# First layer of a four-layer attention program: the maximum ahead of the other VectorE work of its step, and statistics, inverse root, masks and input splits cut up and moved to other steps

## What is computed

```
def _masked_instance_norm(x, mask):
    m = mask.astype(x.dtype)
    x = x * m
    n_valid = jnp.sum(m, axis=-1, keepdims=True)
    mean = jnp.sum(x, axis=-1, keepdims=True) / n_valid
    var = jnp.sum(x * x, axis=-1, keepdims=True) / n_valid - mean * mean
    x = (x - mean) / jnp.sqrt(jax.nn.relu(var) + EPS)
    return x * m
q, k, v = Wq x + bq, Wk kv + bk, Wv kv + bv        (per batch, split into 16 heads)
attn = softmax over the valid keys of (q * scale) k
mean = attn v;  ex2 = attn (v * v);  std = sqrt(relu(ex2 - mean * mean))
out = (masked_instance_norm(x) * std + mean) * mask
```

## Time and profile before

| | us |
|---|---|
| median of 3 runs | 4968.74 |
| the 3 runs | 4964.92 to 4970.57 |
| the profiled execution, its own time | 4961.53 |
| its span, first to last instruction | 4959.9 |
| first layer in that span, to the first transfer of the second | about 955 |
| TensorE busy in the span | 4443.2 (90%) |
| VectorE, ScalarE, GpSimd busy | 3016.6, 1930.0, 1658.7 |

### The profile page before, as it was taken

One profiled execution on the slowest core, in us unless ns is written; L12 is line 12 of the kernel. 1 busy time (PEld: TensorE's weight loads), 2 busy tenths in 40 slices (PEclk: granted clock), 3 DMA queues, 4 the chain that ended last, 5 costly groups with the idle time before them and its releaser, 6 DMA issues. The chain is left out here.

```text
span 4959.9 us, 72439 instructions
## 1 busy us (share of the span) xinstructions
PE 4443.2 (90%) x22864; PEld 3277.2 (66%) x22864; DVE 3016.6 (61%) x6430; ACT 1930.0 (39%) x3756; POOL 1658.7 (33%) x1103
## 2 busy tenths in 40 slices
PE   6999999578888888767999999999999999999986
PEld 3444444255666666545879779787787887888864
DVE  5555555146666766635757567576675766757642
ACT  2444444211222222114545435454254552555511
POOL 1222223234444444322232442333433334333340
PEclk8999998778899889878999999999999999999999
DMA  1000000200000000002222231222312122221123
GB/s 36 23 18 27 18 18 14 98 5 9 14 14 1 14 14 9 9 9 89 63 71 63 66 101 56 78 61 64 98 61 77 61 68 74 72 73 57 57 68 116
DMA packets 126289, 240.90 MB, mean 49 GB/s; under 512 B 16884, under 2 KB 38132, under 8 KB 124896
## 3 DMA queue, kind: packets, MB, share of 16 engines
q1 hardware_dynamic: 123744, 229.50, 14.7%
q0 software_dynamic: 2304, 8.39, 0.4%
HBM read 220.79 MB, written 16.78 MB: 48 GB/s over the span
## 5 line engine op out<-in xcount | busy, mean ns | idle before, releaser
L1790 POOL TENSOR_TENSOR c_wl<-c_wr,c_wh 128x512 fp32r<-128x512 f32 (+1 forms) x576 | 822.6, 1440 | 1674.3 <-ACT c_wh L2102 1466.5
L1355 POOL TENSOR_TENSOR b_sb<-b_sb,b_rt 128x1024 f32<-128x1024 f32 x128 | 285.0, 2226 | 490.1 <-DVE b_sb L1395 490.1
L2196 ACT ACTIVATE c_pr<-c_ps,c_nms 128x257 f32<-128x257 f32 x512 | 244.2, 477 | 477.1 <-DVE c_nms L2390 475.0
L572 ACT ACTIVATE a_ex<-a_ps 128x1024 f32<-128x1024 f32 x256 | 261.2, 1023 | 346.3 <-PE a_ps L408 346.0
L1395 DVE TENSOR_TENSOR_SCAN b_sb<-b_wt,b_s,b_ps 128x256 f32<-128x256 f32 x512 | 355.8, 731 | 11.7 <-issue 4.0
L666 DVE TENSOR_REDUCE a_nm<-a_ps 128x2 f32<-128x1024 f32 x256 | 310.8, 1218 | 76.2 <-PE a_ps L385 73.2
L1849 PE MATMUL c_ps<-c_hh,c_wh 128*128 128x512 f32 x768 | 318.8, 415 | 35.2 <-POOL c_hl L1796 35.2
L1849 PE MATMUL c_ps<-c_gh,c_wh 128*128 128x512 f32 x768 | 307.3, 400 | 20.5 <-DVE c_gl L2428 17.5
L2102 ACT ACTIVATE c_wh<-c_wr 128x512 fp32r<-128x512 f32 (+1 forms) x464 | 316.4, 688 | 9.1 <-PE c_ps L1851 7.5
L1849 PE MATMUL c_ps<-c_wh,c_cth 128*128 128x256 f32 x1024 | 304.6, 297 | 9.3 <-DVE c_ctl L2343 5.0
L1851 PE MATMUL c_ps<-c_hh,c_wl 128*128 128x512 f32 x768 | 310.9, 405 | 0.0
(11 more groups left out here) (306 smaller groups left out, 10925.0 us busy)
## 6 DMA issues: line engine op xcount, KB each, us to landing
c_wr<-in_downs SPq DMA_DIRECT2D x192, 256.0 KB, 2.6
c_wr<-in_wv SPq DMA_DIRECT2D x64, 512.0 KB, 3.9
c_wr<-in_wk SPq DMA_DIRECT2D x128, 256.0 KB, 2.9
c_wr<-in_wq SPq DMA_DIRECT2D x128, 256.0 KB, 2.6
c_wr<-in_fc SPq DMA_DIRECT2D x64, 256.0 KB, 2.8
b_w<-in_w SPq DMA_DIRECT2D x8, 1024.0 KB, 13.1
a_x<-in_x SPq DMA_DIRECT2D x8, 512.0 KB, 3.4
a_ctx<-in_ctx SPq DMA_DIRECT2D x8, 512.0 KB, 4.1
```

The lines of the kernel that those rows point to most:

```text
L572: act.activation(EX[:, n % 4, :, :], ps[:, BT + 2 * (n % 2):BT + 2 * (n % 2) + 2, :], ACT.Exp).then_inc(ex_ready, 1)
L1355: pool.tensor_tensor(SB[:, quad % 3, :, 0:L], SB[:, quad % 3, :, 0:L], RT[:, scan % 2, q // 4, :].unsqueeze(1).broadcast_to([P, 4, L]), AL ...
L1790: pool.tensor_tensor(piece(WL, slot), piece(WR, slot), piece(WH, slot), ALU.subtract).then_inc(piece_cut[slot], 1)
L2196: act.activation(PR[:, i, 0:L + 1], ps[:, BS + 1 - i % 2, 0:L + 1], ACT.Exp, bias=NMS[:, i:i + 1], scale=float(K2) ** -0.5, accum_out=RS[: ...
```

## The change

It has five parts, all in `layer0`. The computation is the same.

1. **Order in a step on VectorE.** `take_max` comes first in every step, ahead of `turned_maxima`.
2. **Statistics.** `moments` keeps only the two operations that read PSUM and stands at step 0 of group 3, before `take_max`; the four that follow become `spread_of_x`, at the end of that step.
3. **Inverse root and spread.** `inverse_root` leaves step 5 of group 0 and is cut in two halves of 128 columns, at step 7 of group 0 and step 0 of group 1. GpSimd multiplies by the spread (`spread_out`, now with a wait of its own on `std_ready`) before it multiplies by the inverse root (`scale`). The lift to zero is done group by group.
4. **Masks.** `mask_rows` moves from step 0 of group 1 to steps 5 and 6 of group 0, half the columns each; the count becomes `count_valid`, at step 1 of group 1; `mask_x` moves from step 5 of group 1 to its step 7 and step 0 of group 2.
5. **Input halves.** One pair of signals for x and ctx becomes two pairs. ScalarE rounds x at step 7 of group 0 and ctx at step 0 of group 1 (before: steps 0 and 1 of group 1). GpSimd takes the low half of x, then scales, then the low half of ctx, then shifts and masks. The projection of queries waits for x alone, that of keys for ctx and the mask row.

The diff, cut to its core:

```diff
-            def cut_low(b):
-
-                pool.wait_ge(xc_high, b + 1 + AHEAD)
+            def cut_x(b):
+
+                pool.wait_ge(x_high, b + 1 + AHEAD)
                 pool.sem_inc(passed, 1)
-                pool.tensor_tensor(XL[:, :, :], X[:, :, :], XH[:, :, :], ALU.subtract)
-                pool.tensor_tensor(CL[:, :, :], C[:, :, :], CH[:, :, :], ALU.subtract).then_inc(xc_low, 1)
+                pool.tensor_tensor(XL[:, :, :], X[:, :, :], XH[:, :, :], ALU.subtract).then_inc(x_low, 1)
+
+            def cut_c(b):
+                pool.wait_ge(c_high, b + 1 + AHEAD)
+                pool.sem_inc(passed, 1)
+                pool.tensor_tensor(CL[:, :, :], C[:, :, :], CH[:, :, :], ALU.subtract).then_inc(c_low, 1)
                 pool.drain().then_inc(inputs_read, 1)
...
-                if g == G0 - 1:
-                    pool.tensor_scalar(VAR[:, :, :], VAR[:, :, :], 0.0, None, ALU.max).then_inc(var_v, 1)
-                    pool.drain()
+                pool.tensor_scalar(VAR[:, :, cols], VAR[:, :, cols], 0.0, None, ALU.max).then_inc(var_v, 1)
...
             def spread_out(b):
+                pool.wait_ge(std_ready, b + 1 + AHEAD)
+                pool.sem_inc(passed, 1)
                 pool.tensor_tensor(XM[:, :, :], XM[:, :, :], VAR[:, :, :], ALU.mult)
...
-            def group_0(b, prior):
+            def group_0(b, prior, more=True):
                 copy_values(b, 1)
                 if prior is not None:
                     group_moments(prior, G0 - 1)
-                    finish_batch(prior)
-
-            def group_1(b, prior, more=True):
+                    spread_out(prior)
                 if more:
-                    cut_low(b + 1)
+                    cut_x(b + 1)
+                if prior is not None:
+                    scale(prior)
+                if more:
+                    cut_c(b + 1)
+
+            def group_1(b, prior):
+                if prior is not None:
+                    shift(prior)
+                    mask_out(prior)
                 copy_values(b, 2)
                 group_moments(b, 0)
...
                 if g == 0:
-                    pe.wait_ge(xc_high, b + 1 + AHEAD)
-                    pe.wait_ge(xc_low, b + 1 + AHEAD)
-                    pe.wait_ge(mask_ready, b + 1 + AHEAD)
+                    pe.wait_ge(x_low, b + 1 + AHEAD)
...
                 it = b * G0 + g
+                if g == 0:
+                    pe.wait_ge(c_low, b + 1 + AHEAD)
+                    pe.wait_ge(mask_ready, b + 1 + AHEAD)
...
-            def group(b, g, left=3, prior=None, first=False):
+            def group(b, g, left=3, prior=None, first=False, more=True):
                 it = b * G0 + g
                 for n in range(NT):
                     act.wait_ge(t_ps, it * NT + n + 1 + AHEAD)
...
                     if g == 1 and left > 2 and n == 0:
-                        cut_x(b + 1)
-                    if g == 1 and left > 2 and n == 1:
                         cut_c(b + 1)
...
                     if g == 0 and n == 5 and prior is not None:
                         roots(prior)
+                    if g == 0 and n == 7 and more:
+                        cut_x(b + 1)
...
-                act.wait_ge(var_v, b + 1 + AHEAD)
+                act.wait_ge(var_v, (b + 1) * G0 + AHEAD)
...
+            def mask_rows(b, half):
+
+                cols = slice(half * L, (half + 1) * L)
+                if half == 0:
+                    dve.wait_ge(inputs_in, (b + 1) * N_IN + AHEAD)
+                    dve.wait_ge(k_ps, b * G0 + AHEAD)
+                mm = dve.tensor_scalar(MBRR[:, cols], M8R[:, cols], -NEG, NEG, ALU.mult, ALU.add)
+                if half == 1:
+                    mm.then_inc(mask_ready, 1)
+
+            def count_valid(b):
                 dve.tensor_reduce(NV[:, :], M8R[:, :], AX.X, ALU.add)
                 dve.drain().then_inc(mask_read, 1)
...
+            def mask_x(b, half):
+
+                if half == 0:
+                    dve.wait_ge(stats_x_in, (b + 1) * N_STATS + AHEAD)
+                    dve.wait_ge(out_ready, b + AHEAD)
+                    dve.tensor_copy(MCOL[:, :], M8C[:, :])
+                    dve.drain()
+                for c in range(2 * half, 2 * half + 2):
                     dve.tensor_scalar(XM[:, c, :], XT[:, c, :], MCOL[:, c:c + 1], None, ALU.mult)
-                dve.drain().then_inc(stats_in, 1)
-                dve.sem_inc(stats_read, 1)
+                if half == 1:
+                    dve.drain().then_inc(stats_in, 1)
+                    dve.sem_inc(stats_read, 1)
...
             def moments(b):
@@ -712,6 +731,8 @@
                 dve.tensor_scalar(ST[:, 0, :], ps[:, BX, 0:L], RN[:, 0:1], None, ALU.mult)
                 dve.tensor_scalar(ST[:, 1, :], ps[:, BX, L:2 * L], RN[:, 0:1], None, ALU.mult)
                 dve.drain().then_inc(st_read, 1)
+
+            def spread_of_x(b):
                 dve.tensor_tensor(ST[:, 2, :], ST[:, 0, :], ST[:, 0, :], ALU.mult)
                 dve.drain()
                 dve.tensor_tensor(ST[:, 2, :], ST[:, 1, :], ST[:, 2, :], ALU.subtract)
@@ -719,14 +740,14 @@
                 dve.tensor_scalar(ST[:, 2, :], ST[:, 2, :], 0.0, None, ALU.max).then_inc(var_x, 1)
                 dve.reciprocal(RN[:, :], NV[:, :])
...
-            def group(b, g, left=3, prior=None, first=False):
+            def group(b, g, left=3, prior=None, first=False, more=True):
                 for n in range(NT):
-                    if g == 1 and left > 2 and n == 0:
-                        mask_rows(b + 1)
+                    if g == G0 - 1 and n == 0:
+                        moments(b)
+                    if left > 1:
+                        take_max(*after(b, g, 2), n)
                     if left and n == TURN_AT:
                         turned_maxima(*after(b, g))
-                    if left > 1:
-                        take_max(*after(b, g, 2), n)
                     if n == OLD_PAIR_AT and not first:
                         if g > 0:
                             take_moments(b, g - 1, 1)
@@ -742,18 +763,35 @@
                         take_moments(b, g, 0)
                     if left and g == G0 - 1 and n == VALUES_AT[1]:
                         take_values(b + 1, 1)
-                    if g == 1 and n == 5:
-                        mask_x(b)
-                    if g == 2 and n == STATS_AT:
-                        moments(b)
-                    if g == 0 and n == 5 and prior is not None:
-                        inverse_root(prior)
-
-            def inverse_root(b):
-                dve.wait_ge(std_ready, b + 1 + AHEAD)
-                dve.reciprocal(ST[:, 3, :], ST[:, 3, :]).then_inc(rstd_ready, 1)
-
-            mask_rows(0)
+                    if g == 0 and n == 5 and more:
+                        mask_rows(b + 1, 0)
+                    if g == 0 and n == 6 and more:
+                        mask_rows(b + 1, 1)
+                    if g == 0 and n == 7 and prior is not None:
+                        inverse_root(prior, 0)
+                    if g == 1 and n == 0 and prior is not None:
+                        inverse_root(prior, 1)
+                    if g == 1 and left > 2 and n == 1:
+                        count_valid(b + 1)
+                    if g == 1 and n == 7:
+                        mask_x(b, 0)
+                    if g == 2 and n == 0:
+                        mask_x(b, 1)
+                    if g == G0 - 1 and n == 0:
+                        spread_of_x(b)
+
+            def inverse_root(b, half):
+                cols = slice(half * P, (half + 1) * P)
+                if half == 0:
+                    dve.wait_ge(std_ready, b + 1 + AHEAD)
+                mm = dve.reciprocal(ST[:, 3, cols], ST[:, 3, cols])
+                if half == 1:
+                    mm.then_inc(rstd_ready, 1)
+
```

53 lines of the change are left out of this document (24 added, 29 removed).

## The result

| | before | after |
|---|---|---|
| median of 4 runs each, us | 4967.81 (4964.92 to 4970.57) | **4860.61** (4855.27 to 4862.44) |
| ratio, 95% interval | | 0.9782 [0.9767, 0.9796] |
| profiled execution, us | 4961.53 | 4855.27 |
| its span, us | 4959.9 | 4853.4 |
| from the span's start to the first product of the second layer, us | 958.27 | 851.26 |

The kernel is 107 us faster. I had forecast 4876 in a range of 4862 to 4944. All of the gain lies in the first layer: it is 107.0 us shorter in the profiled executions, whose whole spans differ by 106.5.

A forecast was written before the change was run, and what follows sets the result against it. TensorE was taken as the bound, losing time to idle moments and a slow clock; 19.4 + 55.5 + 15 + 3 = 93 us off the median of 4968.7 gave 4876 us, range 4862 to 4944.

The forecast's parts named there:

- 29 short waits: TensorE's waits for VectorE's maximum, mostly 0.72 us in step 2 and 0.57 in step 1 of group 3, go: 19.4 us.
- six hand-overs: Step 7 of group 0 and steps 0 to 3 of group 1 get shorter by 9.2 us, six times: 55.5 us.
- last hand-over: Seven steps go from 30.03 to 16.8 us at full clock; with step 7, 15 us less.
- end of the layer: GpSimd's lift by quarters and the inverse root beside the spread at the layer's end: 3 us less.
- The maximum first: In plain steps, VectorE's maximum starts earlier and the copy fits in idle time, so the 0.72 us gaps go.
- A gap of about 1.1 us remains, from ScalarE: In step 7 of group 0 TensorE still waits for ScalarE's exponential; step 7 takes 3.25 us against 5.26.
- The clock stays up: Likeliest case: the 1.1 us gap brings no slow stretch at the hand-overs, 4876 us; chance 0.58.
- it falls at some: Rival: the clock falls at three or four of seven hand-overs, each costing 8.4 us, about 4906; chance 0.14.
- Both rivals on the clock: Clock still falls at every hand-over, 4941 us, chance 0.19; or at three or four of seven, about 4906, chance 0.14.
- What VectorE must do: Mask row, count, inverse root and mask of x, now beside full-clock steps, counted as nothing; bound 3.5 us.
- The case in which an inverse root waits for GpSimd: Its second half waits for the low half of x; maximum of step 1 0.6 us late, 4 us over seven hand-overs.
- The slower rival: TensorE's projection of keys waits 7.4 us at seven hand-overs for GpSimd's low half of ctx: 4993 us; chance 0.03.

The follow-up runs named there:

- e1: The kernel before with part 1 alone, take_max ahead of turned_maxima in every step: 4940.19 us, ratio 0.9949.
- e4: The changed kernel with turned_maxima ahead of take_max again: 4886.38 us, ratio 0.9843 to the kernel before.
- The sweep: The changed kernel with one, two or three small ScalarE copies behind the roots, lengthening the gap in step 7: 4903.36, 4904.83 and 4917.79 us.
- e2: The kernel before with only the whole inverse root moved from step 5 of group 0 to step 7: 4971.45 us, ratio 1.0021.
- e9: The changed kernel with the whole mask row and the count at step 0 of group 1: 4894.12 us, ratio 0.9853 to the kernel before.
- e14: The changed kernel with two more products, later overwritten, in each batch's statistics: 4867.95 us, ratio 0.9788 to the kernel before.
- e13: The changed kernel with GpSimd doing the old batch's chain first and the low halves behind it: 4922.27 us, ratio 0.9919 to the kernel before.
- e10: The changed kernel again with no edit: 4859.93 us, ratio 0.9782 to the kernel before.
- e3: The changed kernel with both halves of the inverse root back in step 5 of group 0: 4932.73 us, ratio 0.9936 to the kernel before.
- e12: The changed kernel with ScalarE's two roots moved from step 5 of group 0 to step 3: 4854.7 us, ratio 0.9785 to the kernel before.
- e7: The changed kernel with three small ScalarE copies behind the two roots: 4917.79 us, ratio 0.9901 to the kernel before.

## Why the prediction was right, and where it was wrong

| term of the sum | forecast, us | measured, us |
|---|---|---|
| 29 short waits | 19.4 | 27.0 |
| six hand-overs | 55.5 | 57.2 |
| last hand-over | 15 | 15.05 |
| end of the layer | 3 | 3.4 |
| start of the span, up to 100 us | 0 | 4.3 |
| sum | 93 | 107 |

**The failed step is the first term, "together these are worth the 19.4 us of the 29 small waits".** They were worth 27.0, which is 7.6 of the 14 us that the forecast fell short, the largest part of it. I took the price of a wait to be the idle time that the profile shows ahead of the product. Step 2 went from 3.71 us (window below) to 2.73: 0.98 and not 0.72. Step 1 of group 3 went from 3.17 to 2.34: 0.83 and not 0.57. These steps of the kernel before:

```profile
149.04:152.21 3.17, 2.60 (x15) 0.95 (x13) 1.47 (x3) 1.62 (x2) 0.00 (x0) 1.00 0.00 0
234.84:238.55 3.71, 2.99 (x17) 1.29 (x16) 2.63 (x3) 1.33 (x2) 0.00 (x0) 1.00 0.01 2
```

The same place of the changed kernel, timeline:

```profile
215.96 0.28 DVE L693 CAST a_nmT<-a_ps 16x128 fp32r<-16x128 f32 x1
...
216.31 0.40 PE L419 MATMUL a_ps<-a_qh,a_kl 32*128 32x512 f32 x2
216.54 0.41 PE L396 MATMUL a_ps<-a_kh,a_qh 32*128 32x512 f32 x2
216.88 1.08 PE L433 MATMUL a_ps<-a_ex,a_vf 128*64 128x512 f32 x4
```

There the difference can be read. In a row of products each is shown as 0.40 long but the next starts 0.23 later: its shown end is past the moment at which the next could start, and the idle time is counted from that end. And the first product after a gap is shown as 0.49 or 0.50 long, and its successor starts 0.43 behind it (in e1: 300.91 and 301.34), where without a gap it is 0.34 (216.54 and 216.88). The first makes 0.17 us, the second 0.09: together 0.26 for each wait, 7.5 us for 29. I had the right number in my hands: the lengths of whole steps stood in the earlier trace rows, and step 2 against a plain step with the same products would have shown it. I used whole steps for the hand-overs, and those terms came out within 2 us; I used idle time here, and that one didn't. The reverse trial, e4, points the same way: some 20 us of idle time, 26 to 30 us of price.

Point by point otherwise:

- *The maximum first.* Right in mechanism: VectorE's copy now follows at once (215.96), and no wait takes its place. The excess of 0.5 us behind the statistics cost nothing.
- *A gap of about 1.1 us remains, from ScalarE.* Right, 1.13 at all seven. Step 7 took 3.33 us against 3.25.
- *The clock stays up.* Right, with a chance of 0.58, but in part by luck, for the reason was weaker than I took it to be. I argued that 1.1 is nearer to 0.72 than to 1.90. The sweep shows that 1.31 was already followed by slow stretches five times in seven, and e2, e4, e9 and e14 that 1.13 itself is at 12 of 28 hand-overs. The rival "it falls at some", at 0.14, is what these four kernels do; the change itself did not in 14 profiled hand-overs, nor, by their mean granted clock of 0.941 or 0.942, in any of 8 runs. Both rivals on the clock deserved their chances.
- *Steps at full clock.* 7.21 us where I had 7.45 (8.17 less a wait of 0.72): the same undercount again, 0.24 us, which makes 1.4 of the 1.7 us that the six hand-overs gave beyond the forecast.
- *What VectorE must do.* The second half of the mask row took 1.82 us beside the spread and the maximum was in time, as worked out. The case in which an inverse root waits for GpSimd didn't come: its second half (191.90, 0.94 us) ran beside GpSimd's low half of x (190.36 to 192.75) but for its last 0.1 us and took what the first took. The Trainium skill, page "SBUF — State Buffer", section "SBUF: two separate sides", has VectorE and GpSimd exclude each other in modes with two ports; by the trace the mask row behaves so (1.82 us, to 0.14 us after the spread's end), the inverse root doesn't.
- *GpSimd's chain.* The spare time was there: no projection waits. e2 and e13 show what that spare time rests on: where the low halves stand behind the old batch, the projection waits some 8 us at each of two hand-overs and 7 at each of six. The slower rival was a real mechanism, disarmed by part 5.
- *The end of the layer.* 3.4 us against 3: inverse root and spread side by side, shown here in the changed kernel:

```profile
827.15 2.34 POOL L260 TENSOR_TENSOR a_xm<-a_xm,a_var 128x1024 f32<-128x1024 f32 x1 [1.27 <-ACT a_var L615]
827.00 1.76 DVE L787 RECIPROCAL a_st<-a_st 128x128 f32<-128x128 f32 x2 [4.15 <-ACT a_var L615]
```

- *The start.* 4.3 us that I hadn't counted come from one slow stretch of 6.8 us and another like it, before 65 us, where the kernel before has 23.9. The first in the windows of the changed kernel:

```profile
40.60:47.40 6.80, 5.70 (x14) 2.72 (x14) 6.58 (x6) 0.00 (x0) 0.00 (x0) 0.50 0.00 0
```

  The second profile of the same kernel (e10) has 23.9 there, and its median is 4859.93 all the same: chance of one execution, not the change. The table adds up the profiled pair, 106 us apart by their own times; e10's median, without this piece, is 105 us below its own before.
- *The range.* Its low end, 4862, left 14 us below the forecast, 4 of them for the end of the layer, and none for a term sized from short idle times. A term of 29 equal waits, each possibly wrong by the same third, is an error that adds up; it belonged into the bounds.

**What stays open.** What decides, at a gap of 1.13 us, whether the clock falls: e9 and e14 show that a second gap isn't needed for it, no run here shows what is. The batch's length alone does not explain e9, whose four runs all have a lower mean clock (0.933 to 0.938), while four of e14's six keep 0.941 with a batch as long. Whether the change keeps its clock in every run is known for 8 runs only. Part 2 was not tried by itself; that the gap of 0.57 us in step 1 of group 3 is its work is read from e1, which has part 1 alone and keeps that gap. The later place of the mask of x, and the inverse root in two halves rather than whole at step 7, were not tried by themselves either.

## What to carry to other kernels

Price a short wait of TensorE by the length of the whole step with and without it, not by the idle time ahead of one product; here that was 0.98 against 0.72 us. Where a slow stretch follows a gap at the same place each time, the gap's price is the stretch's, so first find which engine ends the gap, then which comes next once it is gone, and whether the work that hid beside slow steps still fits beside fast ones. And leave room: here a copy of 0.2 us at one place, in a kernel that had just kept its clock, cost 43 us.

## What the runs showed of the hardware

The granted clock is far more sensitive than I had thought: in a layer in which TensorE is otherwise busy throughout, single gaps of 1.31 us were followed by a stretch at 0.50 in five of seven cases, and the stretch shown went on for 17.10 us although TensorE was busy in all of them. At 1.13 us the outcome varied between executions and hand-overs: 0 of 14 in the changed kernel and 0 of 7 in e13, where the clock fell only in the later wait, but 12 of 28 in e2, e4, e9 and e14. A longer gap does not decide it alone either: in e1 the clock outlived 1.90 us at four of seven hand-overs, where in the kernel before and in e3 it fell at all seven.

The clock also makes runs of one kernel differ: in e14 the four runs with a mean granted clock of 0.941 lie within 4.5 us, the two with 0.936 and 0.933 are 20 to 40 us longer. Kernels that keep it at every hand-over spread little (e12 over 3.7 us). Those that lose it can too (e7 and e13 over 3.2 and 0.6 us), but the kernel before, on the chip of e7, spread over 19 us.

ScalarE pays 1.28 us for a table load and nothing more that the trace shows: the load starts 0.02 us after the end of the operation before it, and the activation behind it 0.01 us after the load's (187.29 to 187.30). The Trainium skill, page "ScalarE: Activation LUTs", section "What ACT_TABLE_LOAD costs", gives some 1.38 us of drain beside it; an estimate from that page's figure, for the two switches, would put the gap near 4 us, and it was 1.13.
